# An attention and expert block with row maxima ahead of the residual statistics, and a new order of loads, copies and zero-fill in its first four steps

## What is computed

```python
x = x + _layernorm(attn(_layernorm(x)))       # attn: a local and a global branch, 16 heads each
x = x + _layernorm(ffn(_layernorm(x)))        # 32 experts, top 1, capacity 320 tokens each

def attn(x):
    local_out  = mha over windows of 128 rows (x @ proj_local),  mask added: +1 above the diagonal
    global_out = mha over windows of 256 rows (x @ proj_global), the same mask
    fused = w[0] * local_out + w[1] * global_out       # w = softmax(fusion_w)
    return _layernorm(fused) * ln_gamma + ln_beta

def _mha(x, W_in, b_in, W_out, b_out, mask):
    q, k, v = split(x @ W_in.T + b_in)
    a = softmax(q @ k.T / 4 + mask)
    return (a @ v) @ W_out.T + b_out
```

## Time and profile before

| | |
|---|---|
| median of 3 runs | 1685.04 us (1684.78 to 1686.82) |
| the profiled execution, its own time | 1684.44 us |
| its span from the first to the last instruction | 1682.7 us |
| busy share of the span: TensorE, VectorE, ScalarE, GpSimd | 90%, 74%, 54%, 43% |
| mean granted TensorE clock | 0.96 |
| first transpose of step 0 | at 31.88 us |
| first transpose of step 1, 2, 3, 4, 5 | at 57.09, 93.52, 141.02, 182.78, 222.70 us |
| a later step | 39.99 us |

### The profile page before, as it was taken

The page is one execution under the profiler, slowest core; times in us unless marked ns, Lnnn a source line. Parts: engine busy times, 40 slices in busy tenths (PEclk is TensorE's granted clock), DMA queues, the critical chain, the costliest instruction groups (busy, mean ns, idle before and its releaser), DMA issues.

```text
span 1682.7 us, 39867 instructions
## 1 busy us (share of the span) xinstructions
PE 1513.9 (90%) x13672; PEld 1095.7 (65%) x13672; DVE 1244.4 (74%) x3785; ACT 914.0 (54%) x1919; POOL 725.6 (43%) x1097
## 2 busy tenths in 40 slices
PE   5569999999999999999999999999999872999993
PEld 3346776676766767777777777766777552777772
DVE  2346888888888878878888888888887742688883
ACT  1235666666666666666666666666666542222220
POOL 1111444444444444444444444444444333366666
PEclk8789999999999999999999999999999985999997
DMA  4997466766666666666666566666666302355540
GB/s 108 191 201 140 83 106 107 107 104 102 103 100 100 101 103 103 101 101 104 98 104 105 103 105 103 103 104 106 102 97 96 93 27 88 104 163 178 175 133 11
DMA packets 253512, 183.56 MB, mean 109 GB/s; under 512 B 29284, under 2 KB 251943, under 8 KB 253310
## 3 DMA queue, kind: packets, MB, share of 16 engines
q1 hardware_dynamic: 244126, 176.22, 57.5%
q0 software_dynamic: 6912, 3.73, 0.8%
q10 hardware_dynamic: 2272, 1.06, 0.3%
HBM read 55.78 MB, written 38.04 MB: 56 GB/s over the span
## 4 chain that ended last, share of the span: by engine, by line
PE 64%; POOL 11%; DVE 9%; issue 8%; SPq 5%; DMA 1%; ACTq 1%; ACT 1%; POOLq 0%; DVEq 0%
PE bank L1242 13%; PE bank L1389 8%; PE bank L1348 7%; PE bank L1224 4%; SPq L406 4%; PE bank L1232 4%; PE bank L1273 4%; PE bank L1270 3%; PE bank L1211 3%; DVE bst L817 3%; POOL rstd L526 3%; PE bank L1203 3%; PE bank L1199 3%; POOL slots_scratch L581 2%; POOL xrow L592 2%
## 5 line engine op out<-in xcount | busy, mean ns | idle before, releaser
L881 DVE TENSOR_REDUCE mx<-bank 128x2 f32<-128x512 f32 (+1 forms) x768 | 516.8, 674 | 170.3 <-PE bank L1270 90.2
L667 ACT ACTIVATE pt<-bank 128x512 f32<-128x512 f32 x768 | 450.7, 594 | 295.4 <-PE bank L1211 171.0
L1242 PE MATMUL bank<-xnT,weff 128*128 128x256 f32 x1024 | 257.8, 396 | 13.8 <-DVE rest L865 13.1
L1242 PEld LDWEIGHTS bank<-xnT,weff 128*128 128x128 f32 x1024 | 188.7, 194 | 50.2 <-DVE rest L865 15.3
L1273 PE MATMUL bank<-stack 96*128 96x256 bf16 x1024 | 197.7, 275 | 5.6 <-DVE mx L881 5.3
L1211 PE MATMUL bank<-stack 100*128 100x128 bf16 x2048 | 198.8, 219 | 0.0
L548 POOL TENSOR_TENSOR parts<-rest,parts 128x512 bf16<-128x512 f32 x128 | 147.1, 1159 | 115.4 <-ACT parts L684 115.4
L678 ACT ACTIVATE parts<-bank,bqk 128x256 bf16<-128x256 f32 x256 | 107.5, 471 | 136.4 <-PE bank L1242 126.2
L559 POOL TENSOR_TENSOR obuf<-obuf,xrow 128x512 f32<-128x512 f32 x32 | 40.6, 1270 | 326.4 <-ACT obuf L709 326.4
L1211 PEld LDWEIGHTS bank<-stack 100*128 100x128 bf16 x2048 | 158.6, 97 | 12.9
L1208 PE MATMUL bank<-tri,identb 128*128 128x256 bf16 x512 | 141.0, 275 | 20.0 <-DMA stack<-mT 18.2
(11 more groups left out here) (152 smaller groups left out, 2754.9 us busy)
## 6 DMA issues: line engine op xcount, KB each, us to landing
stack<-parts SPq DMA_DIRECT2D x384, 128.0 KB, 5.9
stack<-parts SPq DMA_DIRECT2D x768, 64.0 KB, 2.6
slots_scratch<-zeros SPq DMA_DIRECT2D x5, 2080.0 KB, 12.5
xr<-x SPq DMA_DIRECT2D x32, 256.0 KB, 8.7
out<-obuf SPq DMA_DIRECT2D x32, 256.0 KB, 2.2
ew<-w_gate SPq DMA_DIRECT2D x32, 256.0 KB, 4.0
ew<-w_up SPq DMA_DIRECT2D x32, 256.0 KB, 5.2
ew<-w_down SPq DMA_DIRECT2D x32, 256.0 KB, 4.4
```

Of the source, the lines that this page charges most:

```text
L667: act.activation(pt[:, u % 8, :], S2[u % 2][:, :], ACT.Exp).then_inc(p_ready, 1)
L881: dve.reduce_max(dst, src, AX.X).then_inc(s1_read, 1)
L1242: last = pe.matmul(bank[:, t * WIN:(t + 1) * WIN], weff[:, b, c, qk * D + t * P:qk * D + (t + 1) * P], xnT[:, par, c, :], start=(c == 0), ...
```

## The change

It does five things.

1. In VectorE's slots 22 and 23 `maximum` comes first. `stats(3)` moves to slot 23 behind it (`DVE_AT["stats_x1"]` is 23 now), `moments(3)` to slot 0 of the next step (`"moments_x1": 0`).
2. The ScalarE queue issues six loads before the first normalisation, not 38. The 32 loads of `bv` and `wo` go to step 1, two in each of slots 8 to 23; `gamma`, `beta` and the router weights leave SyncE's queue for ScalarE's at the start of step 2. `winT` is loaded in halves, and TensorE's fold takes, for each branch, the first half of its four products first.
3. The output bias leaves the start of the program: VectorE's part goes to step 2, slot 12, TensorE's to the start of step 3, VectorE's sum to step 3, slot 2.
4. Window 1's statistics, 1/std and normalisation go to the start of step 0 (VectorE slot 1 by `at_x`, which is 16 in all other steps as before, GpSimd's first work of the step, ScalarE slot 4). The six copies of window 0's local k go from SyncE's queue to ScalarE's, in slot 12. The copies of `behind` no longer wait for the fold and the bias.
5. The zero-fill is cut into 16 DMAs instead of 5 and goes from SyncE's queue to ScalarE's: one in each odd slot below 16 of steps 2 and 3.

Cut to its core (small tables, unchanged helpers and the memory of six small tensors, which now live through the whole program, are left out):

```diff
-    ZDMAS = 5
+    ZDMAS = 16
@@ VectorE, in step
                 for k in range(UNITS):
+                    if s[0] is None and s[1] == 2 and k == 12:
+                        out_bias()
+                    if s[0] is None and s[1] == 3 and k == 2:
+                        add_out_bias()
+                    if f and k == DVE_AT["moments_x1"]:
+                        moments(3, f)
...
-                    if first and k == DVE_AT["stats_x"]:
+                    if first and k == at_x:
                         first_stats(nxt, 1 - par)
...
+                    if b:
+                        maximum(k, b)
                     if d and k == DVE_AT["stats_x1"]:
                         wait(dve, x1_ready, d)
                         stats(3, x1[:, 1 - par, :, :], d)
-                    if d and k == DVE_AT["stats_x1"] + 1:
-                        moments(3, d)
-                    if b:
-                        maximum(k, b)
@@ VectorE, before the steps
-            dve.wait_ge(wo_in, 16 * 40)
+            dve.wait_ge(bqk_in, 16 * 2)
...
+            def out_bias():
+
+                dve.wait_ge(wo_in, 16 * 37)
+                dve.wait_ge(fus_exp, 1)
+                dve.tensor_copy(bvb[:, :, :], bv[:, :].unsqueeze(2).to_broadcast([P, 4, P]))
...
+                dve.tensor_tensor(bias_row[:, :], bo[:, 0, :], bo[:, 1, :], ALU.add).then_inc(wo_ready, 1)
@@ ScalarE, before the steps
+            def zero_slots(n):
+
+                act.wait_ge(const_dve, 1)
+                dst = slots_d.rearrange("(p g) f -> p g f", p=P)[:, n * ZREP:min((n + 1) * ZREP, NSLOT // P), :]
+                act.dma_start(dst, zeros[:, :].unsqueeze(1).to_broadcast(list(dst.shape))).then_inc(zeroed, 16)
+
+            def spread_local_key(w, par):
+
+                for part, ready in enumerate((hi_ready, mid_ready, lo_ready)):
+                    act.wait_ge(ready, nth(w, 4, 1))
+                    for g in range(6):
+                        if E_PARTS_K[g] == part:
+                            act.dma_start(stack[HD * g:HD * g + HD, par, 0, 1, :, :, :].rearrange("d h t n -> d h (t n)"),
+                                          parts[:, 1, part, :]).then_inc(spread[1], 16)
@@ ScalarE, in step
+                    if s[0] is None and s[1] == 0:
+                        if k == ACT_AT["mid1"] + 4:
+                            spread_local_key(a, par)
+                    if s[0] is None and s[1] == 2 and k == 0:
+                        other_rows()
+                    if s[0] is None and s[1] == 1 and k >= 8:
+                        out_weights((k - 8) // 8, (k - 8) % 8)
+                    if s[0] is None and s[1] in (2, 3) and k < 16 and k % 2 == 1:
+                        zero_slots((s[1] - 2) * 8 + k // 2)
                     if c:
                         exps(k, c)
...
-                    if a and exists(back(a, -1)) and k == ACT_AT["norm0"]:
+                    if a and exists(back(a, -1)) and k == (4 if num(s) == 0 else ACT_AT["norm0"]):
@@ SyncE
-            sp.wait_ge(w_fold, 8)
-            sp.wait_ge(bias_ps, 1)
-            sp.wait_ge(const_dve, 1)
             sp.wait_ge(const_pool, 1)
...
-                if s[0] is None and s[1] < 3:
-                    for n in range(s[1], ZDMAS, 3):
-                        zero_slots(n)
@@ TensorE, before the steps
-            pe.wait_ge(w_fold_out, 4)
-            pe.wait_ge(wo_ready, 1)
-            for c in range(4):
-                last = pe.matmul(TR[:, 0:D], bvb[:, c, :], wo[:, c, :], start=(c == 0), stop=(c == 3))
-            last.then_inc(bias_ps, 1)
             pe.wait_ge(const_pool, 1)
             pe.wait_ge(w_fold_out, 4)
-            pe.wait_ge(const_dve, 2)
+            pe.wait_ge(const_dve, 1)
+            def out_bias():
+
+                pe.wait_ge(wo_ready, 1)
+                for c in range(4):
+                    last = pe.matmul(TR[:, D:2 * D], bvb[:, c, :], wo[:, c, :], start=(c == 0), stop=(c == 3))
+                last.then_inc(bias_ps, 1)
@@ TensorE, in step
+                if s[0] is None and s[1] == 3:
+                    out_bias()
```

More of the change, by code:

```diff
@@ L553, in step @@
                 nxt = back(s, -1)
+                if num(s) == 0:
+                    pool.wait_ge(ln_rstd[0], 1)
+                    pool.wait_ge(xn_ready, 1)
+                    inv_std(0, nxt)
                 if f:
@@ L572, in step @@
                     low_part(2, a)
-                if a and (nxt[0] is not None or nxt[1] < NW):
+                if num(s) > 0 and a and (nxt[0] is not None or nxt[1] < NW):
                     inv_std(0, nxt)
@@ L644, in _, with out_weights @@
-            act.wait_ge(fus_sem, 1)
-            act.activation(fus_e[:, :], fus[:, :], ACT.Exp, bias=fus_m[:, 0:1]).then_inc(fus_exp, 1)
+            for b, k_ in enumerate((bqk_l, bqk_g)):
+                act.dma_start(bqk[:, b, :], k_).then_inc(bqk_in, 16)
+            act.dma_start(fus[:, :], fusion_w.partition_broadcast(P)).then_inc(fus_in, 16)
+            for b, c_ in enumerate((bo_l, bo_g)):
+                act.dma_start(bo[:, b, :], c_.partition_broadcast(P)).then_inc(wo_in, 16)
+            def out_weights(b, n):
+                o_, v_ = ((woT_l, bv_l), (woT_g, bv_g))[b]
+                h, half = n // 2, n % 2
+                lo, at = 64 * half + HD * h, 32 * h + HD * half
+                act.dma_start(bv[at:at + HD, 2 * b:2 * b + 2], v_[lo:lo + HD, :]).then_inc(wo_in, 16)
+                act.dma_start(wo[at:at + HD, 2 * b:2 * b + 2, :], o_.rearrange("(c p) n -> p c n", p=P)[lo:lo + HD, :, :]
+                              ).then_inc(wo_in, 16)
@@ L647, in _ @@
+            for q in range(2):
+                last = act.activation(xn[:, q, :], xw[:, 0, q, :], ACT.Identity, bias=mr[:, 0, q:q + 1], scale=rstd[:, 0, q:q + 1])
+            last.then_inc(xn_ready, 1)
             n = 0
@@ L710, in norm_again @@
                 last.then_inc(o_norm, 1)
-            first_norm((None, 0), 0)
+            act.wait_ge(fus_sem, 1)
+            act.activation(fus_e[:, :], fus[:, :], ACT.Exp, bias=fus_m[:, 0:1]).then_inc(fus_exp, 1)
+            act.wait_ge(bqk_ready, 1)
             def maxima_out(b, a):
@@ L1060, in step @@
                         moments(2, d)
-                    if first and k == DVE_AT["stats_x"]:
+                    if first and k == at_x:
                         first_stats(nxt, 1 - par)
-                    if first and k == DVE_AT["stats_x"] + 1:
+                    if first and k == at_x + 1:
                         moments(0, nxt)
+                    if b:
+                        maximum(k, b)
                     if d and k == DVE_AT["stats_x1"]:
@@ L1344, in step @@
                                 wait_read(pe, TR_USES, "op", s, 1)
+                                if s[0] is None and s[1] == 3:
+                                    pe.wait_ge(const_dve, 2)
                                 wait(pe, onT_ready[0], d, 2, 1)
```

100 lines of the change are left out of this document (47 added, 53 removed).

## The result

| | before | after |
|---|---|---|
| median (lowest to highest) | 1684.91 us (1684.78 to 1686.82) | 1636.07 us (1627.86 to 1638.47) |
| ratio, with its 95% interval | | 0.9699 (0.9663 to 0.9735) |
| the profiled execution, its own time | 1684.44 us | 1638.02 us |
| its span | 1682.7 us | 1636.3 us |
| first transpose of step 0, 1, 2, 3, 4 | 31.88, 57.09, 93.52, 141.02, 182.78 us | 20.32, 35.04, 70.30, 114.87, 153.08 us |

The forecast was 1639 us. The total hides that the parts came out otherwise: step 4 starts 29.7 us earlier (forecast 22.7), and the late steps give 17.55 us (forecast 23.5). The rest of the program, from the start of step 31 on, is 0.85 us longer.

The account below looks back on a forecast made before the run. TensorE's instruction stream was taken to bound late steps, the DMA engines steps 1 to 3. 1684.44 - 12.2 - 1.5 - 12 + 3 - 23.5 = 1638.2, with the median 0.6 higher: 1639 us; 8-in-10 range 1618 to 1660.

Parts of the forecast that it names:

- The maxima, per step: Steps 4 to 31: TensorE's 1.23 us wait goes, 0.39 us returns waiting for the maxima copy; 28 x 0.84 = 23.5 us won.
- Before step 0: Program start: with fewer loads ahead, the fold becomes the chain and the first transpose comes near 19.7 us; -12.2 us.
- Step 0 into 1: The 5.54 us wait for window 1's normalisation goes, copies of k cost 4 before step 1's first scores; -1.5 us.
- Steps 1 to 3: Moving the zero-fill wins 12 of 24 us, the steps staying DMA-bound; the output bias costs 3 us; loads cost nothing.
- (a): Late steps: copies of maxima are not late, all 1.23 us stay won; 11 us less, 1628 us; chance 0.2.
- (b): Steps 1 to 3: the zero-fill costs the same wherever issued, nothing is won there; 1651 us; chance 0.2.
- (c): Late steps win nothing, as ScalarE's later normalisation delays exponentials and TensorE stands as long as before; 1662 us; chance 0.1.
- (d): Steps 2 and 3: the 16 zero DMAs hold ScalarE 6.4 us each; 75 us lost, 1714 us; chance 0.04.

Follow-up runs that it names:

- the earlier copy: The change with SyncE issuing the copy of the global maxima three copies earlier: 1608.11 us, ratio 0.9560; on another chip 1618.55 us, ratio 0.9634.
- The kernel with loads in ScalarE's gaps: The change with 16 of the 32 small loads of bv and wo issued before step 0, in ScalarE's two idle gaps: 1633.80 us, ratio 0.9716.
- the zero-fill's experiment: The change with the zero-fill as before, five DMAs on SyncE's queue at the ends of steps 0, 1 and 2: 1651.09 us, ratio 0.9808.
- the maxima part alone: The kernel before with only VectorE's end of step changed, maxima ahead of statistics and moments: 1663.73 us, ratio 0.9885.

## Why the prediction was right, and where its parts were not

**The maxima, per step.** The mechanism was right: the 1.23 us went at every step, the statistics stopped waiting, and the copy of global maxima became late. The size was too good: 17.55 us where 23.5 stood. The term that was mis-sized is the wait in slot 8, put at 0.39 us a step. Over the 28 steps it is 0.58 us on the mean: 21 of them wait for over 0.2 us, up to 1.36, and 0.76 on the mean. The step from 663.03 to 704.64 is 41.61 us long and lost some 1.7 us more at a lower clock.

The issue time of 10.73 us into the step, from which the 0.39 was worked out, was no odd one: the mean is 10.79 in the change. But the landing took 2.87 us on the mean and not 2.77, and a mean hides the rest. The copy is issued 9.9 to 11.6 us into the step, and one that lands early wins nothing to set against one that lands late. I wrote as the case against rival (a) that SyncE's pace does not change. The trace of the kernel before shows that it does, at 9.92 to 12.41 us over the same 28 steps, and in the step that starts at 583.20 TensorE had already waited for this copy:

```profile
595.61 0.75 SPq L411 DMA_DIRECT2D stack<-mT  x1
```
```profile
598.62 0.28 PE L1208 MATMUL bank<-tri,identb 128*128 128x256 bf16 x1 [0.91 <-DMA stack<-mT]
```

A second size was off and did no harm. The step without a wait is 38.60 us, not the 38.8 that 40.0 - 1.23 gives, and a step with a wait in slot 8 is some 0.17 us longer than its wait says. Both are of the same size: such a wait costs about 0.17 us more than the matmul's row shows (at 637.36 that row has 0.83 us, the one of its weight load 1.00). It stood on both sides of the subtraction. Step 32 did not stay as it was either: its wait grew from 1.33 to 2.64 us. That the wait is the queue's doing is shown by the earlier copy, which brings steps 4 to 30 to 38.60.

**Before step 0.** Forecast -12.2, measured -11.56. The fold ended at 19.68 instead of 18.8, and the first transpose follows it by 0.64 us, not 0.9.

**Step 0 into 1.** Forecast -1.5, up to the first scores of step 1; measured -15.97 there, which is 4.4 us beyond the first transpose's 11.56. The copies of keys cost 6.36 us, not 4. But step 0 itself shrank from 25.21 to 14.72 us, by 10.5: besides the wait of 5.54, its four groups of products fell to 1.99 us each. Before they had been

```profile
33.65 3.46 PE L1242 MATMUL bank<-xnT,weff 128*128 128x256 f32 x8 [0.69 <-ACT xnT L737]
38.95 2.73 PE L1242 MATMUL bank<-xnT,weff 128*128 128x256 f32 x8 [1.84 <-DVE rest L865]
43.52 3.65 PE L1242 MATMUL bank<-xnT,weff 128*128 128x256 f32 x8 [1.84 <-DVE rest L865]
49.00 2.54 PE L1242 MATMUL bank<-xnT,weff 128*128 128x256 f32 x8 [1.84 <-DVE rest L865]
```

12.38 us, now 7.96. This term is missing from my sum: 4.4 us of clock. The granted clock of step 0 was 0.64 and is 1.00. Before, TensorE was busy for 3.78 of the 10.46 us from the end of the fold to 31.80; now it comes from the fold with 0.64 us idle between. The kernel with loads in ScalarE's gaps lies between: 3.29 us idle, and a granted clock of 0.90 in step 0.

**Steps 1 to 3.** Forecast -12 + 3 = -9 for the zero-fill and the bias; from the first scores of step 1 to the start of step 4 it is 124.81 before and 111.08 after, -13.7. The waits of slot 8, which I had at 6 and 5 us, are 0.72 and 1.15. Two things stand against that. The 32 loads, priced at nothing because ScalarE is idle in step 1, run over into step 2 with the three others and hold TensorE for 3.26 us, and 1.7 more at the lower clock; with 16 or 24 of them moved away the wait is gone. The output bias costs 2.02 us and 1.5 at the lower clock beside TensorE's own part. The zero-fill's move (queue, step and cut together) was worth 20.9 us on the chip, near the 20.1 us of waits that I had read, and over the 12 that I let be won; my sum of DMA time (42 us of load in 38 us) made steps 2 and 3 tighter than they were: their shares of 0.81 and 0.87 are 36 and 33 us.

**The rivals.** (a) fell: the copies are late, though the earlier copy shows its 38.6 us steps. (b) fell by the zero-fill's experiment. (c) fell: ScalarE's wait for the norm's scale grew from 20.9 to 46.0 us, and no late step of TensorE waits for ScalarE. (d) fell: the 16 issues took ScalarE 0.37 to 0.53 us each.

So that the total came within 3 us is luck: two errors cancel, 7 us too little at the start (the clock of step 0, slot 8 of steps 2 and 3) and 6 us too much in the late steps.

## What to carry to other kernels

When a wait of an engine is removed, look for the transfer that it had covered, and read its issue time over many steps, not in one: here one slow issue among the 13 small DMAs ahead of the urgent one decides whether a step waits. Moving the urgent one three places up was worth 22.1 us on top, more than the 19.4 us of the removed wait itself, and nothing without it. Do not put large DMAs between small urgent ones on one queue: here the first copy behind a pair of them took 6.4 to 9.2 us to issue. Where several waits end close together, an edit that removes one may win nothing, so look for the next wait before you judge it.

## What the runs showed of the hardware beyond that

- The granted clock can fall after a wait of about 1 us in a stretch that is otherwise full, and mostly it does not. In the step that starts at 663.03 it fell after the wait of 1.15 us at 677.29, with no other wait in sight, and the step took 1.7 us more than others with such a wait. After the 1.36 us at 597.76 it stayed at 1.00. One step of 41.5 or 41.6 us stands in two more traces, behind 1.02 us (the maxima part alone) and 1.27 us (the zero-fill back on SyncE's queue). What decides it stays open.

```profile
676.00:680.00 4.00, 2.85 (x14) 2.25 (x12) 1.55 (x7) 2.46 (x5) 2.58 (x3) 0.72 0.30 99
680.00:685.00 5.00, 5.00 (x44) 3.83 (x44) 2.08 (x9) 0.68 (x2) 0.91 (x1) 0.88 0.68 147
```

- SyncE issues one of these small DMAs mostly in 0.55 to 0.62 us, now and then in 1.2 to 2.0, and the copy of maxima in 0.75. Behind a pair of large zero DMAs the first one takes 6.38 to 9.19 us and the next ones soon 0.6 again. ScalarE's queue took 2.25 and 2.17 us for two small loads before step 0 and 0.33 to 0.51 us for the 14 others.
